# One class per row in the neighbour search, the second layer norm's centring and scaling on ACT, and one more chunk summed in pairs on DVE

## What is computed

```python
h = jnp.maximum(_layernorm(x), 0.0)
x = x + (tanh([h, t] @ W1 + b1) @ W2 + b2) + adj @ XB - jnp.sum(adj, axis=1, keepdims=True) * XB   # XB = h @ B.T
h = jnp.maximum(_layernorm(x), 0.0)
scores = leaky_relu(a_self[:, None] + a_neigh[None, :]) - 1e10 * (1.0 - adj)       # per head
x = x + relu(softmax(scores) @ (h @ W) + bias)
```

## Time and profile before

| | |
|---|---|
| median of 3 runs | 792.81 us (790.75 to 794.08) |
| the profiled execution, its own time | 791.36 us |
| its span, first to last instruction | 789.6 us |
| PE, DVE, ACT, POOL busy | 87%, 83%, 75%, 49% of the span |
| moved by DMA | 287.02 MB, 363 GB/s on average |

### The profile page before, as it was taken

How to read it: one execution, slowest core, us unless ns; L and a number is a source line. 1 busy time by engine, 2 the same in 40 slices (tenths; PEclk the granted TensorE clock), 3 DMA queues, 4 the chain that set the end, 5 groups by cost and what they waited for, 6 DMA issues and landing times.

```text
span 789.6 us, 13173 instructions
## 1 busy us (share of the span) xinstructions
PE 684.5 (87%) x4470; PEld 244.7 (31%) x4470; DVE 652.1 (83%) x944; ACT 594.3 (75%) x507; POOL 388.5 (49%) x281
## 2 busy tenths in 40 slices
PE   4899999999999999999999999999999999992100
PEld 1233333333333233333333333323233333332000
DVE  4586899999999989989899999999988989893420
ACT  3798888898879798888888887979797878880200
POOL 7000544434170807051443526070888888887574
PEclk9999999999999999999999999999999999995555
DMA  8999899999999999999999999999999999951161
GB/s 329 415 417 430 340 429 395 420 397 422 399 403 432 377 429 377 432 375 432 375 423 399 424 389 415 431 376 430 366 423 388 427 392 411 416 200 28 35 122 20
DMA packets 34544, 287.02 MB, mean 363 GB/s; under 512 B 7456, under 2 KB 13968, under 8 KB 18016
## 3 DMA queue, kind: packets, MB, share of 16 engines
q1 hardware_dynamic: 23168, 275.00, 84.4%
q0 software_dynamic: 9056, 9.73, 4.9%
...
HBM read 279.46 MB, written 7.34 MB: 363 GB/s over the span
## 4 chain that ended last, share of the span: by engine, by line
PE 34%; DMA 27%; DVE 16%; issue 15%; ACT 3%; POOL 3%; DVEq 1%; SPq 0%; POOLq 0%; ACTq 0%
DMA ring<-in_adj_t 26%; PE acc L1032 22%; DVE work L742 6%; PE row_sums L1040 4%; PE row_sums L1050 4%; DVE work L731 4%; ACT work L544 2%; POOL out L499 2%; DVE work L738 1%; POOL work L490 1%; DVE work L748 1%; DVE idx_cls L769 1%; PE ps_xb L1080 1%; PE ps_acc L1073 1%; DMA work<-agg_dram,late_from 1%
## 5 line engine op out<-in xcount | busy, mean ns | idle before, releaser
L544 ACT CAST work<-ring 128x4096 f16<-128x4096 f32 x128 | 458.6, 3603 | 64.4 <-DMA ring<-in_adj_t 26.3
L1032 PE MATMUL acc<-ring,x_pb 128*64 128x512 f32 x2048 | 455.9, 596 | 14.8 <-DMA ring<-in_adj_t 14.8
L447 POOL DMA_INDIRECT cand<-in_adj,cls_row x128 | 226.7, 1771 | 86.9 <-DVE cls_row L773 49.0
L742 DVE TENSOR_TENSOR work<-work 128x4096 f16<-128x4096 f16 x96 | 221.6, 2309 | 22.5 <-ACT work L544 19.5
L1032 PEld LDWEIGHTS acc<-ring,x_pb 128*64 128x64 f32 x2048 | 140.4, 137 | 318.2 <-issue 280.1
L731 DVE TENSOR_TENSOR work<-ring 128x2048 f32<-128x2048 f32 x90 | 208.8, 2334 | 8.0 <-DMA ring<-in_adj_t 3.6
...
L461 POOL DMA_INDIRECT gathered<-agg_dram,best x64 | 85.5, 1336 | 20.9 <-issue 20.9
L1050 PE MATMUL row_sums<-work,ones_cols 128*32 128x512 f32 x720 | 89.5, 598 | 0.2 <-DVE work L731 0.2
L1040 PE MATMUL row_sums<-ring,ones_cols 128*32 128x512 f32 x608 | 72.9, 616 | 14.0 <-DMA ring<-in_adj_t 14.0
L436 POOL TENSOR_TENSOR x_tq<-x_tq,b_row 128x256 f32 (+1 forms) x16 | 30.4, 1902 | 42.5 <-DMA x_tq<-in_x 42.3
L738 DVE TENSOR_TENSOR work<-work 128x4096 f16<-128x4096 f16 x16 | 36.6, 2286 | 2.3 <-ACT work L544 2.3
...
## 6 DMA issues: line engine op xcount, KB each, us to landing
ring<-in_adj_t SPq DMA_DIRECT2D x128, 2048.0 KB
...
cand<-in_adj,cls_row POOLq DMA_INDIRECT x128
...
gathered<-agg_dram,best POOLq DMA_INDIRECT x64
```

The source lines that it names most:

```text
L447: pool.indirect_dma_start(out=cand[:, k, g * NB:(g + 1) * NB], out_offset=None, in_=classes, in_offset=bass.IndirectOffsetOnAxis(ap=cls_ro ...
L544: act.copy(half_chunk[c % 2], slot(c)).then_inc(half_done, 1)
L742: dve.tensor_tensor(half_max, half_max, half_chunk[c % 2], ALU.max).then_inc(max_done, 1)
L1032: last = pe.matmul(acc[0][at:at + D, :], x_pb[:, c * CB + b, :], slot(c)[:, b * W:(b + 1) * W], start=(c == 0 and b < 2), stop=(c == NC - ...
```

## The change

It has three parts.

1. For the rows of strips 0 to 13 (`SURE` = 14) POOL fetches only the best class, 4 transfers per strip. `search_candidates` scans 64 numbers in place of 128; where the second class might hold a larger number (`bound`, from its fp16 maximum, is not below the largest found) the row is marked `unsure` and `best` becomes N or more, a row of zeros that is added to `agg_dram`. After the loop `unsure_rows` picks one such row per partition, POOL fetches both its classes, and `resolve_unsure` works out the true neighbour, which joins the late rows. The last two strips are searched with both classes (`search_both`). `WINDOWS` gets other limits, and POOL's last window another order: the `unsure` fetches, `store_agg`, all 8 class fetches of the last strip, 4 gathers.
2. `cen` is not made any more: ACT squares x1 with the negated mean as its bias, and scales with `rstd` and a bias `shift` (a new `scale_h1` on ACT, between the casts of chunks 6 and 7). DVE's `scale_h1` makes only `rstd` and `shift`.
3. Chunk 4 is in `PAIRED`: DVE adds its halves, and PE sums 4 in place of 8 matmuls for it. With 7 pairs a strip and 2 buffers, the first pair of a strip uses the buffer of the last one before.

The flag at the end checks a few numbers more. The diff, cut to its core:

```diff
-PAIRED = (0, 1, 2, 5, 6, 7)
+PAIRED = (0, 1, 2, 4, 5, 6, 7)
...
-WINDOWS = ((11, 0, 14), (12, 14, 28), (13, 28, 42), (14, 42, 56), (15, 56, 60))
+WINDOWS = ((11, 0, 12), (12, 12, 28), (13, 28, 46), (14, 46, 56), (15, 56, 60))
...
+SURE = 14
+KEPT = SURE * TB
...
-        agg_dram = nc.dram_tensor("agg_dram", (N, D), F32, kind="Internal").ap()
+        agg_dram = nc.dram_tensor("agg_dram", (N + P, D), F32, kind="Internal").ap()
...
+            pool.dma_start(agg_dram[N:N + P, :], agg[:, 0:D]).then_inc(zero_stored, 16)
...
-            def fetch_rows(k0, k1):
+            def fetch_rows(k0, k1, cls=1):
                 for k in range(k0, k1):
-                    for g in range(CLS):
+                    for g in range(cls):
...
-            for w, (known, t0, t1) in enumerate(WINDOWS):
-                if known + 1 < S:
-                    add_b2(known + 1)
-                fetch_candidates(known, 0, TB // 2)
+            for w, (known, t0, t1) in enumerate(WINDOWS[:-1]):
+                cls = 1 if known < SURE else CLS
+                add_b2(known + 1)
+                fetch_candidates(known, 0, TB // 2, cls)
                 if w:
                     pool.wait_ge(got[w - 1], 16 * (WINDOWS[w - 1][2] - WINDOWS[w - 1][1]))
                 store_agg(known - 1)
-                if known < S - 1:
-                    fetch_rows(TB // 2, TB)
+                fetch_rows(TB // 2, TB, cls)
                 pool.wait_ge(agg_stored, 16 * known)
                 gather(w, t0, t1)
-            fetch_rows(TB // 2, TB)
+            pool.wait_ge(unsure_row_done, 1)
+            for g in range(CLS):
+                pool.indirect_dma_start(
+                    out=unsure_cand[:, g * NB:(g + 1) * NB], out_offset=None, in_=classes,
+                    in_offset=bass.IndirectOffsetOnAxis(ap=unsure_row[:, g:g + 1], axis=0),
+                ).then_inc(unsure_in, 16)
+            w = len(WINDOWS) - 1
+            pool.wait_ge(got[w - 1], 16 * (WINDOWS[w - 1][2] - WINDOWS[w - 1][1]))
+            store_agg(S - 2)
+            fetch_candidates(S - 1, 0, TB, CLS)
+            pool.wait_ge(agg_stored, 16 * (S - 1))
+            gather(w, WINDOWS[w][1], WINDOWS[w][2])
             pool.wait_ge(agg_last_stored, 16)
...
-                act.wait_ge(h1_centred, s + 1)
+                act.wait_ge(mean_done, s + 1)
                 for k in range(TB):
-                    act.activation(tmp[:, k, :], cen[:, k, :], ACT.Square, accum_out=stat[:, 2, k:k + 1]).then_inc(var_done, 1)
+                    act.activation(tmp[:, k, :], x_tq[:, bass.ds(s * TB + k, 1), :].rearrange("q a d -> q (a d)"), ACT.Square,
+                                   bias=stat[:, 1, k:k + 1], accum_out=stat[:, 2, k:k + 1]).then_inc(var_done, 1)
...
+            def scale_h1(s):
+                act.wait_ge(scale_done, 2 * s + 2)
+                act.sem_inc(act_past, 1)
+                for k in range(TB):
+                    act.activation(h1[:, k, :], x_tq[:, bass.ds(s * TB + k, 1), :].rearrange("q a d -> q (a d)"), ACT.Identity,
+                                   bias=shift[:, k:k + 1], scale=rstd[:, k:k + 1]).then_inc(h1_done, 1)
...
                 deviation_h1(s - 1)
                 halve(s, 6)
+                scale_h1(s - 1)
                 halve(s, 7)
...
-                dve.wait_ge(pair_used, s * NPAIR + (i - PBUF + 1))
+                dve.wait_ge(pair_used, s * NPAIR + max(i - PBUF + 1, 0))
...
-                dve.scalar_tensor_tensor(cls_step[:, :], idx_cls[:, :, 1], -1.0, idx_cls[:, :, 0], ALU.add, ALU.subtract)\
-                    .then_inc(cls_step_done, 1)
...
+            def search(s, n):
+                for k in range(TB):
+                    dve.max(top_cand[:, k, :], cand[:, k, 0:n]).then_inc(cand_top, 1)
+                dve.wait_ge(cand_top, s * TB + TB)
+                dve.sem_inc(dve_past, 1)
+                for k in range(TB):
+                    dve.max_index(idx_cand[:, k, :], top_cand[:, k, :], cand[:, k, 0:n]).then_inc(cand_done, 1)
+                dve.wait_ge(cand_done, s * TB + TB)
...
-                dve.wait_ge(cand_in, s * (16 * TB * CLS) + 16 * TB * CLS)
+                dve.wait_ge(cand_in, s * (16 * TB) + 16 * TB)
...
-                dve.scalar_tensor_tensor(at_second[:, :], idx_cand[:, :, 0], float(NB), cls_step[:, :], ALU.is_ge, ALU.mult)\
-                    .then_inc(pick, 1)
+                search(s, NB)
+                dve.tensor_scalar(bound[:, :], top_cls[:, :, 1], 1.0 + ROUND, FLOOR, ALU.mult, ALU.add).then_inc(pick, 1)
                 dve.scalar_tensor_tensor(in_class[:, :], idx_cls[:, :, 0], float(NB), idx_cand[:, :, 0], ALU.mult, ALU.add)\
                     .then_inc(pick, 1)
-                dve.wait_ge(pick, s * 2 + 2)
+                dve.scalar_tensor_tensor(classes_of[:, ts], idx_cls[:, :, 0], float(P), idx_cls[:, :, 1], ALU.mult, ALU.add)\
+                    .then_inc(pick, 1)
+                dve.wait_ge(pick, s * 4 + 3)
+                dve.tensor_tensor(unsure[:, ts], bound[:, :], top_cand[:, :, 0], ALU.is_ge).then_inc(pick, 1)
+                dve.wait_ge(pick, s * 4 + 4)
+                dve.sem_inc(dve_past, 1)
+                dve.scalar_tensor_tensor(best[:, ts], unsure[:, ts], float(N), in_class[:, :], ALU.mult, ALU.max)\
+                    .then_inc(best_done, 1)
+            def search_both(s):
...
+            def unsure_rows():
+                dve.wait_ge(best_done, SURE)
+                dve.wait_ge(pool_const, 17)
+                dve.tensor_tensor(unsure_key[:, :], classes_of[:, :], span_t[:, :], ALU.add).then_inc(unsure_chain, 1)
+                dve.tensor_reduce(good[:, 6:7], unsure[:, :], AX.X, ALU.add).then_inc(unsure_chain, 1)
+                dve.wait_ge(unsure_chain, 2)
+                dve.tensor_tensor(unsure_key[:, :], unsure_key[:, :], unsure[:, :], ALU.mult).then_inc(unsure_chain, 1)
...
+                dve.scalar_tensor_tensor(unsure_row[:, :], unsure_node[:, :].to_broadcast([P, CLS]), float(P), unsure_cls[:, :],
+                                         ALU.mult, ALU.add).then_inc(unsure_row_done, 1)
...
+            def resolve_unsure():
+                dve.wait_ge(unsure_in, 16 * CLS)
+                dve.max(unsure_lead[:, :], unsure_cand[:, :]).then_inc(unsure_chain, 1)
+                dve.scalar_tensor_tensor(unsure_step[:, :], unsure_cls[:, 1:2], -1.0, unsure_cls[:, 0:1], ALU.add, ALU.subtract)\
...
-                dve.tensor_scalar(stat[:, 1, :], stat[:, 0, :], -1.0 / D, None, ALU.mult).then_inc(chain, 1)
-                dve.wait_ge(chain, c0 + 4)
-                dve.tensor_tensor(cen[:, :, :], x1, wide(stat[:, 1, :], TB), ALU.add).then_inc(h1_centred, 1)
+                dve.tensor_scalar(stat[:, 1, :], stat[:, 0, :], -1.0 / D, None, ALU.mult).then_inc(mean_done, 1)
...
-                dve.reciprocal(rstd[:, :], stat[:, 3, :]).then_inc(h1_done, 1)
-                dve.wait_ge(h1_done, 2 * s + 1)
-                dve.tensor_tensor(h1[:, :, :], cen[:, :, :], wide(rstd[:, :], TB), ALU.mult).then_inc(h1_done, 1)
+                dve.reciprocal(rstd[:, :], stat[:, 3, :]).then_inc(scale_done, 1)
+                dve.wait_ge(scale_done, 2 * s + 1)
+                dve.tensor_tensor(shift[:, :], stat[:, 1, :], rstd[:, :], ALU.mult).then_inc(scale_done, 1)
...
                 fold_chunk(s, 3)
+                add_pair(s, 4)
                 add_pair(s, 5)
                 residual(s - 1)
...
             add_bias(S - 2)
-            search_candidates(S - 2)
+            unsure_rows()
+            search_both(S - 2)
             search_classes(S - 1)
             residual(S - 1)
-            scale_h1(S - 1)
...
+            resolve_unsure()
+            scale_h1(S - 1)
+            n = len(WINDOWS) + 2
+            dve.wait_ge(unsure_done, 1)
+            dve.wait_ge(late_chain, n - 1)
+            dve.scalar_tensor_tensor(late_key[:, 0:KEPT], unsure[:, :], unsure_move[:, :], late_key[:, 0:KEPT], ALU.mult, ALU.add)\
...
-                pe.wait_ge(h1_done, 2 * s + 2)
+                pe.wait_ge(h1_done, s * TB + TB)
...
                 paired_sums(s, 2)
-                for c in (3, 4):
-                    sums(c).then_inc(pe_chunk, 1)
+                sums(3).then_inc(pe_chunk, 2)
+                paired_sums(s, 4)
                 paired_sums(s, 5)
```

119 lines of the change are left out of this document (98 added, 21 removed).

## The result

| | before | changed |
|---|---|---|
| median of its runs, us | 791.78 (789.52 to 794.08, 4 runs) | 817.55 (811.79 to 823.69, 4 runs) |
| profiled execution, its own time | 791.36 | 813.85 |
| its span | 789.6 | 812.1 |
| first to last mark of `runmax` (15 strips) | 642.85 | 669.57 |
| last mark to the end | 78.0 | 74.2 |

The ratio is **1.035, 95% interval 1.031 to 1.039: slower**, and by more than forecast. One of the four executions of the changed kernel, 811.79, lies inside the forecast range, the median does not. In a later job the changed kernel took 812.8 beside 786.0, ratio 1.033 (1.031 to 1.036). The kernel before is some 5 us faster there than in the first measurements, so times are compared only within one job from here on.

A forecast was written before the change was run, and what follows sets the result against it. DVE's serial order was taken as the bound: 2.21 - 0.09 - 0.45 - 0.22 = +1.45 us a strip, fifteen strips +21.8, less 6.6 of waits, +15.2, end 0; median near 807.5 us, range 796 to 812.

The forecast's parts named there:

- DVE's serial order is the period: Strip loop: DVE's instruction order sets the 42.42 us strip, so DVE changes count one for one outside two hand-overs.
- One class, gain 0 and cost 0: `search_candidates` between folds 1 and 2: finishing earlier only lengthens DVE's 0.98 us wait; gain 0, cost 0.
- Pair of chunk 4, +2.21, and the waits of chunk 5 gone, -6.6: DVE: one more `add_pair`, +2.21 us a strip; chunk 5 waits (5.9) and small waits (0.7) vanish over the loop.
- `cen`, -0.45: DVE, negated mean to `rstd`: without `cen` the next fold, ACT's squares and `rstd` come earlier, -0.45 us a strip.
- `h` to `shift`, -0.22: DVE after `rstd`: the 0.34 us product `h` becomes a 4-number `shift` with a step of 0.12, -0.22 us a strip.
- Loop +15.2: Fifteen strips at +1.45 us make +21.8; less 6.6 of vanished waits, +15.2 us (from +12 to +21).
- End 0: After the loop: 2.5 us of `unsure_rows` hidden under unexplained idle time, POOL stays ahead; change 0.
- The stall: At the end: 18.8 us no row explains, between PE's last `ps_xb` matmul and ACT's copy of `acc_tq`; hides `unsure_rows`.
- a changed wait for `acc_tq`: Sign of error at the end: forecast had `acc_tq` copied 19 us after `ps_xb`; a changed wait would show it wrong.
- Rival 2: Loop grows by 15 and the end's stall goes; POOL then decides; median 794 to 797 us, chance 0.20.
- Rival 1: Strip loop: the stream or PE is the bound, so faster: 788 us or 779 us; chance 0.08.
- Rival 3: Loop: chunk 7's cast late behind `scale_h1`, or the chunk 5 waits don't go; 813 to 822 us, chance 0.08.

The follow-up runs named there:

- the kernels with filled waits: Kernel before with chunk 2's pair between folds 1 and 2 (780.8 us) or fold 5 before the reciprocal (783.8); both, in the changed kernel without pairing: 773.9.
- the changed one with both moves: Changed kernel with chunk 2's pair between the folds of chunks 1 and 2, and chunk 5's fold ahead of the reciprocal: 792.1 us, ratio 1.0074.
- the first experiment: Pairing of chunk 4 alone, put into the kernel before: 812.0 us, ratio 1.0331.

## Why the prediction was wrong

It said 807.5, range 796 to 812, slower at 0.80. The direction, the bound and the main term were right, the sum was too small: +1.45 us a strip forecast, +2.40 measured. Of the 10 us between 807.5 and the median of 817.55, 6.3 are in the profiled execution (813.85); the other 3.7 are the spread of the four executions.

- *DVE's serial order is the period*: right. The pairing alone gives 2.14 us a strip though TensorE and the DMA queues are fuller. The rule on occupancy that it weighed, from the Trainium skill (Perfetto Trace Analysis, "Identifying the Most-Contended Engine"), would have named the stream; it would have been wrong for this change. A third to half a microsecond further on the stream or TensorE does hold the strips, as the kernels with filled waits show; which of the two, no run says.
- *One class, gain 0 and cost 0*: right between the folds (6.24 us from fold to fold in both). It moved something the step didn't look at: four fetches less on GpSimd bring `add_b2` forward. Of GpSimd's queue inside the loop the prediction says nothing.
- *Pair of chunk 4, +2.21, and the waits of chunk 5 gone, -6.6*: right, +2.20, and the loop of the pairing alone grew by 25.8 where these two terms make 26.6.
- *`cen`, -0.45 (bounds -0.35 and -0.6)*: **the step that failed**, the largest of four misses. It let `rstd` come earlier by all that the squares start earlier, at the squares' old price, in a form that now carries a pointer. (ACT's four scalings, priced at 0.9 us, took 1.34 to the next cast; that was hidden.) Measured -0.04, outside the bounds: the path from the mean to `rstd` runs over ACT, and taking work off DVE beside it only lengthens the wait. The fold behind the mean did start 0.35 earlier, the lower bound, but `rstd` did not follow it.
- *`h` to `shift`, -0.22*: mis-sized, -0.04. The large fold behind a dependent small instruction starts 0.30 after it, not 0.12; the 0.25 between the negated mean and `cen` in the same stretch would have told.
- *GpSimd's addition*: left out altogether, although the 2.82 us pair stood in the strip that was read. +0.21 a strip, and shown by the kernel without it.
- *The top of the strip*: +0.16, not foreseen. It is there in the changed kernel, in that without `b2`, in that with one class alone, and in the changed one with both moves; it is absent without the pairing and in the kernels made from the one before. No part explains it alone; open.
- *Loop +15.2*: +26.7. The four misses make 0.41 + 0.18 + 0.21 + 0.16 = 0.96 in a steady strip. Over fifteen that would be 14.4; 11.5 appeared. The first three strips lost only 0.54 each beyond the forecast, and in the last four GpSimd's addition costs neither kernel its 0.75 or 0.54 (0.39 once in the changed one). These two make some 2 us of the difference; the rest was not followed up.
- *End 0*: -3.8 between the two traces, -1.2 between the two without a stall. The stall, named there as the cover for `unsure_rows`, was 14.0 us and not 18.8 in the measured execution and is absent from the later one. The prediction had named a changed wait for `acc_tq` as a sign that it was wrong; it changed, and the end got shorter all the same, so 0 for it was close by luck.
- *Rival 2* was wrong about the size, not the mechanism: the stall did go in the later executions, and the end got 2 to 5 us shorter. That GpSimd's queue then decides holds for the kernel before, and only in part for the changed one. Its 794 to 797 needed more than 10. *Rival 1* fell with the first experiment. *Rival 3*, 813 to 822, has the measured time, by neither of its two mechanisms: the cast of chunk 7 was on time and the waits went.
